# Cross-attention block: one gathered reciprocal per tile, spread by transfers, in the place of one per head group

## The reference

```python
q = split_heads(x @ Wq.T); k = split_heads(text @ Wk.T); v = split_heads(text @ Wv.T)
probs = softmax(q @ k.T * 32**-0.5, axis=-1)      # over the 77 context rows
out_text = merge_heads(probs @ v)
# the second context, rows 77 and up, is empty here: its term adds nothing
out = out_text @ Wo.T + bo + x
```

## Time and profile before

| | us |
|---|---|
| median of 3 runs | 476.56 |
| lowest and highest | 473.17, 476.89 |
| span of the profiled execution | 472.5 |
| PE (TensorE matmul) busy | 444.0 |
| DVE (VectorE) busy | 390.6 |
| ACT (ScalarE) busy | 327.4 |
| POOL (GpSimd) busy | 230.9 |

### The profile page before, as it was taken

The page is one execution under the profiler, slowest core; times in us unless marked ns, Lnnn a source line. Parts: engine busy times, 40 slices in busy tenths (PEclk is TensorE's granted clock), DMA queues, the critical chain, the costliest instruction groups (busy, mean ns, idle before and its releaser), DMA issues.

```text
span 472.5 us, 8672 instructions
## 1 busy us (share of the span) xinstructions
PE 444.0 (94%) x2538; PEld 316.6 (67%) x2538; DVE 390.6 (83%) x508; ACT 327.4 (69%) x633; POOL 230.9 (49%) x186
## 2 busy tenths in 40 slices
PE   8969988799899998999899998999899998999997
PEld 6857655467676766767576766676676766667765
DVE  0556998898989987898989889888989888898783
ACT  1759888867677784867678785868677775857620
POOL 5603685644547372544537373545446372532440
PEclk9999989999999998999999999999999998999999
DMA  8994422435344442444344453445344543334302
GB/s 282 397 229 139 113 74 74 114 90 163 96 123 131 121 154 77 149 113 146 100 131 132 122 154 113 112 121 172 97 121 118 143 126 91 90 91 140 107 24 111
DMA packets 37969, 61.44 MB, mean 130 GB/s; under 512 B 8241, under 2 KB 10033, under 8 KB 37937
## 3 DMA queue, kind: packets, MB, share of 16 engines
q1 hardware_dynamic: 27136, 41.36, 31.2%
q10 hardware_dynamic: 10800, 19.67, 13.1%
HBM read 28.81 MB, written 10.49 MB: 83 GB/s over the span
## 4 chain that ended last, share of the span: by engine, by line
PE 63%; DVE 18%; issue 6%; ACT 5%; SPq 3%; DMA 3%; ACTq 1%; DVEq 0%
PE ps_q L691 21%; PE ps_o L691 19%; DVE rden L566 7%; PE ps_s L739 7%; PE ps_pv L746 5%; PE ps_m L723 4%; DVE x_lo L534 4%; DVE mx L553 3%; PE ps_den L751 3%; ACT x_hi L368 2%; DMA x_f<-in_x 2%; DVE attn L575 1%; ACT p_f L421 1%; PE ps_m L790 1%; SPq L276 1%
## 5 line engine op out<-in xcount | busy, mean ns | idle before, releaser
L318 POOL TENSOR_TENSOR p_lo<-p_f,p_hi 77x512 f16<-77x512 f32 x120 | 146.7, 1229 | 180.3 <-ACT p_hi L425 180.3
L421 ACT ACTIVATE p_f<-ps_s 77x512 f32<-77x512 f32 x160 | 94.6, 591 | 58.9 <-PE ps_s L739 58.8
L566 DVE RECIPROCAL rden<-ps_den 128x256 f32<-128x256 f32 x80 | 134.7, 1720 | 0.4 <-PE ps_den L751 0.4
L425 ACT ACTIVATE p_hi<-ps_s 77x512 f16<-77x512 f32 x160 | 93.5, 584 | 2.0 <-PE ps_den L751 2.0
L553 DVE TENSOR_REDUCE mx<-ps_m 128x4 f32<-128x308 f32 x160 | 68.7, 471 | 21.8 <-PE ps_m L723 21.2
L691 PE MATMUL ps_q<-x_hi,wq_hi 128*128 128x512 f32 x200 | 80.7, 403 | 0.2
L691 PE MATMUL ps_q<-x_lo,wq_hi 128*128 128x512 f32 x200 | 79.6, 398 | 0.0
L691 PE MATMUL ps_q<-x_hi,wq_lo 128*128 128x512 f32 x200 | 79.5, 398 | 0.0
L403 ACT CAST q_packed<-q_hi 32x512 fp32r<-32x512 f32 x120 | 74.0, 617 | 2.4
L691 PE MATMUL ps_o<-attn_hi,wo_hi 128*128 128x512 f32 x170 | 70.9, 417 | 0.0
L691 PE MATMUL ps_o<-attn_hi,wo_lo 128*128 128x512 f32 x170 | 68.2, 401 | 0.0
(11 more groups left out here) (106 smaller groups left out, 614.1 us busy)
## 6 DMA issues: line engine op xcount, KB each, us to landing
x_f<-in_x SPq DMA_DIRECT2D x40, 256.0 KB, 3.2
q_packed<-q_hi SPq DMA_DIRECT2D x160, 64.0 KB, 2.1
q_packed<-q_lo SPq DMA_DIRECT2D x160, 64.0 KB, 2.0
x_res<-in_x ACTq DMA_DIRECT2D x35, 256.0 KB, 2.8
out<-out_sb ACTq DMA_DIRECT2D x35, 256.0 KB, 2.6
wk_sb<-in_wk SPq DMA_DIRECT2D x8, 320.0 KB, 5.8
wv_sb<-in_wv SPq DMA_DIRECT2D x5, 512.0 KB, 10.0
wq_sb<-in_wq SPq DMA_DIRECT2D x5, 320.0 KB, 9.1
```

The lines of the kernel that those rows point to most:

```text
L318: nc.gpsimd.tensor_tensor(p_lo[:, i, :], p_f[:, i, :], p_hi[:, i, :], ALU.subtract).then_inc(plo_pool, 1)
L421: nc.scalar.activation(p_f[:, i, :], ps_s[i % 2][0:L, :], ACT.Exp, scale=SCALE).then_inc(pf_done, 1)
L425: nc.scalar.activation(p_hi[:, i, :], ps_s[i % 2][0:L, :], ACT.Exp, scale=SCALE).then_inc(phi_done, 1)
L566: nc.vector.reciprocal(rden[:, cols], ps_den[:, cols]).then_inc(rden_done, 1)
```

## The change

All of a tile's five groups now add their denominators into one PSUM bank. `ones` becomes six matrices of 77x32: for group g of a tile it has ones only in the columns n with n mod 8 equal to g or to g + 5 below 8, and zeros elsewhere; the sixth is the old one, all ones. So `add_up` writes group g's denominators on the partitions g (and g + 5) of every eight, and the accumulation in `ps_den` runs from the tile's first group to its last. `invert_den` runs once a tile, in step (t, 0) for tile t-1, and writes `rden_rows`. SP's new `spread_rden` issues five transfers, one a chunk: each reads 16 partitions of `rden_rows` (one of every eight) and writes each to 8 partitions of a slot of `rden`, 256 KB written. `rden` has three slots, and takes the memory of `out_sb`; the output is now finished in place in `x_res`, so that the next residual load waits for the store.

VectorE's new `copy_values` moves `ps_pv` times `v_scale` into `attn` at the start of the next step, and `values` waits for that (`pv_copied`) instead of `norm_done`. `normalise` multiplies `attn` by the slot of `rden`, in place: chunks 0 to 3 of tile t-1 at the end of step (t, 0), with `attn_low` 1 behind them, and chunk 4 with `attn_low` 3 in step (t, 1), behind the first two `reduce_max`. The `q_low` of step (t, 0) moves behind these two. ScalarE's `attn_high` 0 stands ahead of `q_high` in step (t, 0), 1 and 2 behind it, 3 and 4 among the exponentials of step (t, 1); GpSimd's `attn_low` 0 is the last of step (t, 0), 2 and 4 the first of step (t, 1). The last tile is done as before: a full inversion for each group, and `normalise` from PSUM.

```diff
-        ones = sb("ones", [L, D], F16)
+        ones = sb("ones", [L, G + 1, D], F16)
-        rden = sb("rden", [P, TB], F32)
+        rden_rows = sb("rden_rows", [P, TB], F32)
-        out_sb = sb("out_sb", [P, RS, TB], F32)
+        rden = sb("rden", [P, RS, TB], F32)
...
+    def ends(t, g):
+        return g == 0 and exists(t) and exists(t - 1)
+    def ended(t, g):
+        return g == 1 and ends(t, 0)
+    def inverts(t, g):
+        return is_last(t) or (g == G - 1 and exists(t))
...
@@ SP @@
+            def spread_rden(t):
+                sp.wait_ge(rden_done, 2 * (t + 1))
+                for c in range(G):
+                    if exists(slot_before(t, c)[0]):
+                        sp.wait_ge(norm_done, nth(*slot_before(t, c)) + 1)
+                    rows = rden_rows[c:P:DS, :].unsqueeze(1).to_broadcast([P // DS, DS, TB])
+                    sp.dma_start(rden[:, c % RS, :], rows).then_inc(rden_in[c % RS], 16)
 ...
                     load_max(*shift(t, g, 1))
+                if ends(t, g):
+                    spread_rden(t - 1)
@@ GpSimd @@
+            nc.gpsimd.memset(ones[:, 0:G, :], 0.0).then_inc(ones_done, 1)
+            nc.gpsimd.memset(ones[:, G, :], 1.0).then_inc(ones_done, 1)
+            for n in range(DS):
+                nc.gpsimd.memset(ones[:, n % G, n:D:DS], 1.0).then_inc(ones_done, 1)
...
+                if ended(t, g):
+                    attn_low(t - 1, POOL_CHUNKS[1:])
                 if xt is not None:
                     x_low(xt, POOL_CHUNKS[:2])
...
+                if ends(t, g):
+                    attn_low(t - 1, POOL_CHUNKS[:1])
@@ ScalarE @@
                     exponentials(t, g, 0)
+                if ended(t, g):
+                    attn_high(t - 1, (3,))
                     exponentials(t, g, 1)
+                if ended(t, g):
+                    attn_high(t - 1, (4,))
...
+                if ends(t, g):
+                    attn_high(t - 1, (0,))
                 if exists(shift(t, g, 2)[0]):
                     q_high(*shift(t, g, 2))
+                if ends(t, g):
+                    attn_high(t - 1, (1, 2))
...
-                    act.wait_ge(outs_done, nth(*slot_before(t, k)) + 1)
+                    act.wait_ge(out_in[k % RS], 16 * slot_uses(*slot_before(t, k)))
                 act.dma_start(x_res[:, k % RS, :], x[t, :, k, :]).then_inc(res_in[k % RS], 16)
...
-                act.dma_start(out[t, k], out_sb[:, k % RS, :]).then_inc(out_in[k % RS], 16)
+                act.dma_start(out[t, k], x_res[:, k % RS, :]).then_inc(out_in[k % RS], 16)
@@ VectorE @@
-                nc.vector.reciprocal(rden[:, cols], ps_den[:, cols]).then_inc(rden_done, 1)
+                nc.vector.reciprocal(rden_rows[:, cols], ps_den[:, cols]).then_inc(rden_done, 1)
...
+            def copy_values(t, g):
+                dve.wait_ge(pv_done, nth(t, g) + 1)
+                free_chunk(t, g)
...
+                nc.vector.tensor_scalar(attn[:, g, :], ps_pv[:, :], v_scale[:, g:g + 1], None,
+                                        ALU.mult).then_inc(pv_copied, 1)
+            def normalise(t, g):
+                if is_last(t):
...
+                dve.wait_ge(pv_copied, G * t + g + 1)
+                dve.wait_ge(rden_in[g % RS], 16 * slot_uses(t, g))
+                nc.vector.tensor_tensor(attn[:, g, :], attn[:, g, :], rden[:, g % RS, :], ALU.mult).then_inc(norm_done, 1)
...
+                if exists(last_t) and not is_last(last_t):
+                    copy_values(last_t, last_g)
                 if exists(shift(t, g, 1)[0]):
                     reduce_max(*shift(t, g, 1), 0)
                     reduce_max(*shift(t, g, 1), 1)
+                if ended(t, g):
+                    normalise(t - 1, 4)
+                    attn_low(t - 1, 3)
+                    q_low(*shift(t, 0, 2))
+                if inverts(last_t, last_g):
+                    invert_den(last_t, last_g, 0)
                 if exists(t):
                     p_low(t, g, 0)
...
-                if exists(last_t):
+                if inverts(last_t, last_g):
                     invert_den(last_t, last_g, 1)
+                if is_last(last_t):
                     normalise(last_t, last_g)
...
+                if ends(t, g):
+                    for c in range(4):
+                        normalise(t - 1, c)
+                    attn_low(t - 1, 1)
+                elif exists(shift(t, g, 2)[0]):
                     q_low(*shift(t, g, 2))
@@ TensorE @@
-                        last = nc.tensor.matmul(ps_den[D * i:D * (i + 1), :], ones[:, :], p[:, i, :],
+                        last = nc.tensor.matmul(ps_den[D * i:D * (i + 1), :], ones[:, G if is_last(t) else g, :],
+                                                p[:, i, :], tile_position=(0, D * i), **flags)
+                first, end = (True, True) if is_last(t) else (g == 0, g == G - 1)
-                if exists(shift(t, g, -1)[0]):
+                if is_last(t) and g >= 1:
                     pe.wait_ge(norm_done, nth(t, g))
+                elif exists(shift(t, g, -1)[0]):
+                    pe.wait_ge(pv_copied, nth(t, g))
+                    if g == 0:
+                        pe.wait_ge(rden_done, 2 * t)
```

72 lines of the change are left out of this document (37 added, 35 removed).

## The result

The changed kernel takes **515.9 us** (median of 4 runs, 514.6 to 517.95), the kernel before, run beside it, 476.6 (4 runs, 473.17 to 476.89): the ratio is 1.085, with a 95% interval of 1.079 to 1.091. I had forecast 500 with a range of 482 to 516. The direction was right; the slowdown of 39 us is 1.7 times the +23 of my sum. As a time the median lies at the very edge of the range, and as a ratio just outside it: 1.085, where 516 over the 476.56 known then is 1.083. The profiled execution took 515.79 with a span of 514.2, 41.7 above the span of before; its mean granted TensorE clock is 0.954.

What follows compares the result with a forecast made beforehand. TensorE, busy for 94% of the span, sets the pace; -3.6 -5.5 +26.4 +6.1 -3.1 +3 = +23, and 472.5 + 23 + 4.1 = 500 us, range 482 to 516.

Steps and rivals of the forecast that it cites:

- steps (t, 3): Six steps that also split the next x: reciprocals ahead of `values` go, the copy delays `reduce_max`; net -3.6 us.
- the two slow steps: Steps (2, 4) and (6, 4), partly at 1.2 GHz, 11.5 instead of 9.96 us: they give back -3.1.
- The q transfers behind SP's spreading: `pack_q` transfers queued behind `spread_rden` land near S+24, read at S+26.3: thin cover of 2 us, no cost summed.
- (c): Tile boundary, steps (t, 0) and (t, 1): transfers in series and DVE's list delay PE; +26.4 us, first boundary +6.1.
- (d): TensorE's clock: two steps give back -3.1 us; half-clock matmuls after four of seven longer waits cost +3.
- DVE's work alone: Rival: without transfer waits DVE's list ends at S+17.2, a pair takes about 21.6; 472 to 478 us, chance 0.09.
- some 510: The sum if every `normalise` beside GpSimd's `attn_low` or `p_low` takes one such operation longer.
- Clock and port: Rival: boundary as forecast, plus a clock drop at each (+8) and crowded `normalise` (+4 to +10); 508 to 520, chance 0.15.
- (b): Start-up, steps (0, 2) to (0, 4), waiting for DVE's `q_top` behind reciprocals: -5.5 us, bounds -2 and -8.
- (e): Parts said to cost nothing: `add_up` matmuls, memsets of `ones`, the last tile inverted as before, storing from `x_res`.

Runs made afterwards that it cites:

- n14: The changed kernel with `copy_values` moved from the head of VectorE's step to behind the second two `reduce_max`: 512.53 us, ratio 1.078.
- n4: The kernel before with 68 of its 80 reciprocals left out, all but the first group's and the last tile's: 454.88 us, ratio 0.956.
- n5: The changed kernel with ScalarE's `q_high` ahead of `attn_high` 0 in step (t, 0): 517.39 us, ratio 1.090.
- n2: The changed kernel with five places for the spread reciprocals, chunks 3 and 4 in `attn_lo`'s memory, all transfers issued at once: 521.47 us, ratio 1.094.
- n13: The changed kernel without spreading transfers and with GpSimd's `attn_low` of tiles 1 to 6 cut to one column: 487.61 us, ratio 1.028.
- n1: The changed kernel with the spreading transfers left out, `normalise` reading `rden_rows` itself: 499.55 us, ratio 1.048.
- n3: The changed kernel with each spreading transfer reading 128 different partitions once instead of 16 partitions eight times: 510.0 us, ratio 1.070.
- n6: The changed kernel with `normalise` 3 moved from step (t, 0) to step (t, 1), behind the first two `reduce_max`: 512.02 us, ratio 1.083.
- n7: The changed kernel with the first half of the inversion moved behind the second two `reduce_max`: 512.44 us, ratio 1.083.
- n12: The changed kernel with five more matmuls in step (t, 1) ahead of the output projection, while TensorE waits: 514.6 us, ratio 1.078.
- n15: The changed kernel with `copy_values` behind the inversion, both inversion halves behind the second two `reduce_max`, and `normalise` 3 late: 496.09 us, ratio 1.039.

## Why the prediction was right in direction and too small

**Right:** that the boundary decides and is dear; that steps (t, 3) win little because the copy stands ahead of `reduce_max` (-4.3 against -3.6; n14 shows the copy, and n4 the whole 1.4 a step that was to be had); that the two slow steps come back (-3.1); the order of the waits in step (t, 1), first `attn_lo` 0 and 1, then `reduce_max`; 24 reciprocals; and that VectorE idles twice for the spreading, though its second idle time lay ahead of chunk 1 and not of chunk 3. TensorE's first wait in step (t, 1) was for `q_high`, 1.18 in the boundary shown, which n5 shows to be covered as I had said, and `reduce_max` was waited for once and not twice. The q transfers behind SP's spreading cost nothing: TensorE waits for one `q_packed` transfer in the whole kernel, 2.8 us, and before it was 3.0. The step is 16 to 17.8 long where I had named 14.7, but step (t, 0) met its 10.4 with 10.75.

**The step that failed is the sum of (c),** 25.1 us a pair where the runs showed 26.75 to 28.5: +48.2 with the first boundary, where (c) had +32.5 and (d) +3. Follow it through the boundary at 201.09. The second reciprocal ended at S+7.96 where I had 7.6: +0.36. The landing, which I took as 2.8 "nearer the one of its own size", was 3.78, from an issue at S+8.1: the first chunk came at S+11.87 and not at 10.5, +1.37 by now. From there to the end of `normalise` 3 it took 4.5 us, as forecast, but not for the reason given: I had put it down to the slot that chunk 3 must wait for, while VectorE idled for chunk 1 (1.38), and n2 shows that with five slots the landings are 1.37 apart all the same. Then came VectorE's own operations, priced uncrowded: `p_low` of 1.5 in the place of 0.7 here, +0.7. The sum, +2.05, is the list's end at S+22.65 where I had 20.6, and 27.1 for 25.1. In the last three pairs VectorE's `attn_low` 1 fell beside GpSimd's too, as in that at 317.45,

```profile
334.23 1.76 DVE L646 TENSOR_TENSOR attn_lo<-attn,attn_hi 128x512 fp32r<-128x512 f32 x1
```

and they are 27.4 to 28.5 long, though chunk 0 came at S+11.3 in two of them.

The causes, taken apart by the runs, for the most frequent pair of each: 19.9 clean (n4); 22.8 with VectorE's new order and only `p_low` crowded (n13); 24.5 with GpSimd's `attn_low` beside it (n1); 26.8 to 28.5 with the transfers (after). By the means of the six pairs it is 19.9, 23.2, 24.9 and 27.4. So of the 7.5 us some 3.3 are the new order with `p_low`, 1.7 GpSimd's `attn_low`, and 2.6 the transfers with what they do to the clock. The parts hold for this order of taking them away; in the kernel after, half of the pairs have no crowded `attn_low`. The first part holds the rival "DVE's work alone", which had the list's end at S+17.2 and a pair at 21.6. It ended at S+18.33 in n13, and what lies between is about the 1.2 us of the two crowded `p_low`, by the estimate above. So the list was right and its prices were not, and the rule on VectorE and GpSimd, which I had set beside the sum at "some 510", belonged in the sum.

**The bounds** of (c) took a landing of 3.2 at most, because 3.2 was the longest row of that size, though it was another kind of transfer, from HBM. n3 shows that the difference is the source: 128 partitions read once land in 2.5, 16 partitions read eight times in 3.7. The measured time lies outside my forecast of 484 to 508 and in the rival "Clock and port", 508 to 520, to which I gave 0.15. That rival had the crowded operations and a clock drop at every boundary, which all seven show, but it kept the short landing, so the runs bear out a part of it and not the whole. That 4.5 us of (c) came out as forecast was luck.

**(b) Start-up,** -5.5 forecast, -0.8 measured. Step (0, 4) gained 0.95 of the forecast 2.0, but (0, 3) grew from 12.18 to 12.57. TensorE waits 2.89 us for `mx` in it, behind two `x_low`, the value scaling and now the copy, and what follows runs at half clock: the granted clock is 0.73 in that stretch where it was 0.86. n14, with the copy behind `reduce_max`, takes 39.55 for the start-up against 41.55, so up to 2.0 of it was the copy's place; n6, whose start-up is that of the kernel after, took 40.56, so 1 us of this differs from one execution to the next.

**(e) Nothing** was wrong for the last tile: (7, 2) and (7, 3) take 10.75 each, since the first half of the inversion was moved ahead of `p_low` and the second two `reduce_max` for this tile too, and the transpose waits for it. n7 moves it back and has 9.94. I had read "as before" off the inversion and not off its place. **(d)** had the right sign. It took four boundaries of seven as followed by half-clock matmuls, and all seven are, at 0.87 to 0.94. Its size can't be separated in the kernel after, where VectorE's list hides part of the half-clock work, and n12 failed to remove it. It is read in one step of n15 alone, 2.8 us, and no run shows that this holds for the kernel after.

**Still open:** how much of the transfers' 2.6 us is the clock. Three of the six pairs of after show a clock of 0.94 and three 0.88, with about 1 us between them. The three at 0.88 are those with `attn_low` 1 at 1.76 in the place of 0.68, and TensorE waited longer there for chunk 1, 1.51 to 2.51 against 0.82 to 1.43, so the 1 us is the crowding and the lower clock goes with the longer wait. Why the crowding falls into these three is not shown.

## What to carry to other kernels

When work is gathered to the end of a tile, its consumer's deadline does not move: write the one list of the engine between the last input and the first use, with every operation at the duration it has beside a busy neighbour, and the transfer as a term of its own. A reciprocal saved is worth nothing where the engine has slack, and a 0.75 us copy put ahead of what TensorE waits for costs its full length in each step that was late already. A late result on the matmul engine is paid twice where the engine comes out of the wait at half clock, as in n15.
